# Spreading one group of a shared feed-forward over the tail of the attention stage

## The reference

```python
x = x + _L0_xattn_ref(_layernorm(x), ctx_512, Wq, Wkv_expand, Wout)      # 16 heads, causal
x = x + _L0_ffn_ref(_layernorm(x), ...)
# inside the feed-forward, xf is (3584, 512)
probs = softmax(xf @ gate_w.T); top_p, top_i = top_k(probs, 2)           # 8 experts
h = silu(xf @ expert_fc1[e].T) * (xf @ expert_fc2[e].T)                  # 352 wide
y = sum over the two chosen experts of top_p * (h @ expert_proj[e].T)
shared = (silu(xf @ shared_fc1.T) * (xf @ shared_fc2.T)) @ shared_proj.T # 1408 wide
y = y + sigmoid(xf @ shared_gate_w.T) * shared
```

## Time and profile before

| what | value |
|---|---|
| median of the runs | 1655.21 us (3 runs, 1654.87 to 1656.95) |
| the profiled execution | 1659.46 us, its span 1657.7 us |
| mean granted clock of TensorE | 0.975 |
| busy: PE, PEld, DVE, ACT, POOL | 94%, 80%, 52%, 37%, 33% |
| attention with its tail | to about 517 us |
| jobs | about 517 to 1004 us |
| shared feed-forward | about 1004 us to the end |

### The profile page before, as it was taken

One profiled execution on the slowest core, in us unless ns is written; L12 is line 12 of the kernel. 1 busy time (PEld: TensorE's weight loads), 2 busy tenths in 40 slices (PEclk: granted clock), 3 DMA queues, 4 the chain that ended last, 5 costly groups with the idle time before them and its releaser, 6 DMA issues.

```text
span 1657.7 us, 32046 instructions
## 1 busy us (share of the span) xinstructions
PE 1558.9 (94%) x11388; PEld 1328.0 (80%) x11388; DVE 860.6 (52%) x1661; ACT 613.0 (37%) x1946; POOL 552.2 (33%) x507
## 2 busy tenths in 40 slices
PE   4999999999833999999999999999999999999998
PEld 4788878888723999999999997888888888888886
DVE  4567667776554666666666664532323223333322
ACT  3778767777702333333333333321111111111111
POOL 4233445554454655556555531101010100000010
PEclk9999999999966999999999999999999999999999
DMA  5233434443324666666666655321120303030110
GB/s 168 76 92 91 91 85 91 89 87 70 85 45 144 235 243 237 238 237 237 245 242 237 237 189 204 128 88 40 47 77 4 109 18 102 25 102 25 51 52 26
DMA packets 82465, 202.71 MB, mean 122 GB/s; under 512 B 37424, under 2 KB 38448, under 8 KB 77648
## 3 DMA queue, kind: packets, MB, share of 16 engines
q1 hardware_dynamic: 70208, 168.44, 31.6%
q0 software_dynamic: 12176, 33.20, 6.2%
HBM read 153.64 MB, written 47.97 MB: 122 GB/s over the span
## 4 chain that ended last, share of the span: by engine, by line
PE 86%; issue 5%; DVE 3%; POOL 3%; DMA 2%; ACT 1%; another core or an unknown queue 0%; DVEq 0%; SPq 0%; POOLq 0%; ACTq 0%
PE psum L567 53%; PE psum L833 13%; PE psum L783 8%; PE psum L665 3%; PE psum L656 2%; PE psum L684 2%; PE psum L756 1%; POOL lists_dram L1071 1%; PE psum L693 1%; PE psum L673 1%; PE psum L716 1%; PE psum L580 1%; DVE wj_lo L1468 1%; DMA wj_raw<-in_w_experts 1%; PE psum L647 1%
## 5 line engine op out<-in xcount | busy, mean ns | idle before, releaser
L1179 POOL DMA_INDIRECT routed<-expert_out_dram,slot_b x56 | 55.3, 987 | 575.5 <-DVE slot_b L1530 383.4
L567 PE MATMUL psum<-nT_hi,ws_hi 128*128 128x512 f32 x616 | 243.2, 395 | 3.6 <-DVE nT_lo L1478 3.6
L567 PE MATMUL psum<-nT_hi,ws_lo 128*128 128x512 f32 x616 | 244.8, 397 | 0.0
L567 PE MATMUL psum<-nT_lo,ws_hi 128*128 128x512 f32 x616 | 244.2, 396 | 0.0
L1517 DVE TENSOR_TENSOR h_s<-psum,silu_s 128x512 f32<-128x512 f32 x77 | 53.3, 692 | 363.9 <-PE psum L567 359.7
L567 PE MATMUL psum<-gT_hi,wj_hi 128*128 128x256 f32 (+1 forms) x840 | 233.1, 278 | 1.2 <-DVE gT_lo L1449 1.2
L567 PE MATMUL psum<-gT_hi,wj_lo 128*128 128x256 f32 (+1 forms) x840 | 232.8, 277 | 0.0
L567 PE MATMUL psum<-gT_lo,wj_hi 128*128 128x256 f32 (+1 forms) x840 | 232.8, 277 | 0.0
L1141 POOL TENSOR_SCALAR wj_hi<-wj_raw 128x2816 fp32r<-128x2816 f32 x68 | 136.7, 2028 | 147.5 <-PE psum L783 102.2
L912 ACT ACTIVATE probs<-psum,minus_max 112x112 f32<-112x112 f32 x512 | 176.3, 432 | 3.1 <-DVE minus_max L1264 3.1
L1468 DVE TENSOR_TENSOR wj_lo<-wj_raw,wj_hi 128x2816 fp32r<-128x2816 f32 x70 | 170.3, 2435 | 7.6 <-POOL wj_hi L1141 4.5
(11 more groups left out here) (193 smaller groups left out, 3300.7 us busy)
## 6 DMA issues: line engine op xcount, KB each, us to landing
wj_raw<-in_w_experts SPq DMA_DIRECT2D x35, 2176.0 KB, 8.7
expert_out_dram<-y_c SPq DMA_DIRECT2D x35, 512.0 KB, 2.7
wj_raw<-in_w_shared SPq DMA_DIRECT2D x11, 768.0 KB, 4.4
x_in<-in_x SPq DMA_DIRECT2D x32, 224.0 KB, 4.0
x_res<-in_x SPq DMA_DIRECT2D x32, 224.0 KB, 3.1
x_dram<-x SPq DMA_DIRECT2D x32, 224.0 KB
normed_dram<-xn SPq DMA_DIRECT2D x32, 224.0 KB, 3.1
normedT_dram<-xn2T SPq DMA_DIRECT2D x32, 224.0 KB, 3.8
```

The costliest lines, as they stand in the source:

```text
L567: mm = pe.matmul(out_ap, u, v, start=(n == 0), stop=(n == last))
L1179: pool.indirect_dma_start(out=routed[:, b % 2, c, :], out_offset=None, in_=expert_out_dram, in_offset=bass.IndirectOffsetOnAxis(ap=slot_b[ ...
```

## The change

Group 0 of the shared feed-forward leaves the last stage. Its eleven chunks go onto TensorE, ScalarE and VectorE as `chunk0(0)` to `chunk0(7)` behind each of the steps (8, 0) to (9, 3), and as chunks 8 to 10 behind the last step. They have the same 24 + 12 matmuls as before, but one PSUM bank for each half of the hidden layer (5 and 7) and single buffers `silu_0` and `h_0`. The weights of each chunk are loaded and split for this group alone, and loaded and split again in the shared stage, whose first group is now group 1. The input of group 0 is loaded and split in the steps (7, 0) to (7, 3), one quarter in each. The result is added to `base0` in the first job, and stored back over the rows of `x1_dram` from which it came.

The table of jobs is made in two parts: `table_first` before chunk 6 and `table_second` after chunk 7. The 13 steps that compared a count with the multiples of 256 one after the other become one comparison over 128 x 104 elements and one sum. The barrier behind attention no longer waits for TensorE. The weights of job 0 are loaded in step (8, 2) into a buffer of their own and split between the chunks 8 and 9. In every step `aT_lo` now comes ahead of `choose` and `place` on VectorE.

The first group of the shared stage (group 1) adds the experts' outputs of two groups: those of group 0 in chunks 2 to 5, and its own, placed in chunk 8, two in chunk 9 and two in chunk 10. Between them SP stores group 0 and loads the `base` of group 1.

The core of the diff, for SP and TensorE:

```diff
+        def first_chunk(g, j):
+
+            return (g - NG) * TB + j if isinstance(g, int) and g >= NG else None
+
+        TAIL_CHUNKS = range(2 * TB, SC)
...
+            for i in range(2):
+                sp.dma_start(w0_raw[i], w_shared[i]).then_inc(w0_loaded[i], 16)
+
+            def load_chunk0(c):
+                if c + 2 < SC:
+                    sp.wait_ge(S["fc0_split"], c + 1)
+                    sp.wait_ge(S["pj0_split"], c + 1)
+                    sp.dma_start(w0_raw[c % 2], w_shared[c + 2]).then_inc(w0_loaded[c % 2], 16)
+
+            def tail_loads(g, j):
+                if g == NG and j == 0:
+                    sp.wait_ge(S["scores_done"], NB)
+                    sp.dma_start(base0[:, :, :], x1_dram[0:ST].rearrange("(b p) c -> p b c", p=P)).then_inc(S["base0_loaded"], 16)
+                    sp.dma_start(route_b0[:, :, :], route_groups[0]).then_inc(S["base0_loaded"], 16)
+                if g == NG and j == 2:
+                    wait_emptied(sp, NG, 1, "proj")
+                    sp.dma_start(wj_raws[0][:, :], w_experts[0]).then_inc(wjraw_loaded[0], 16)
+                load_chunk0(first_chunk(g, j))
 
...
+                    if isinstance(g, int) and g == NG - 1:
+                        if j == 0:
+                            for i in range(2):
+                                sp.wait_ge(x1_stored[i], 16 * 3)
+                                sp.wait_ge(xn2T_stored[i], 16 * 3)
+                            sp.wait_ge(S["route_stored"], 16 * 2)
+                        if j >= 2:
+                            sp.wait_ge(S["n0_split"], j - 1)
+                        sp.dma_start(n0_in[j % 2], normedT_dram[:, j, 0:ST]).then_inc(n0_loaded[j % 2], 16)
                     if j == 1 and before(g, NG - 1):
                         sp.wait_ge(S["ctx_split"], 2 * g + 2)
...
+                    if isinstance(g, int) and g >= NG:
+                        tail_loads(g, j)
...
@@ -472,6 +559,8 @@
                                  route_of(g - 1)[:, :, :]).then_inc(S["route_stored"], 16)
 
             groups(sp, body, 2)
+            for c in TAIL_CHUNKS:
+                load_chunk0(c)
...
             load_ids(0, 0)
             load_ids(1, 1)
-            sp.wait_ge(gathered[0], 16 * JT)
+            sp.wait_ge(S["pj0_split"], SC)
+            sp.wait_ge(S["fc0_split"], SC)
             load_weights(1, 1)
+            sp.wait_ge(S["base0_added"], SB)
+            sp.dma_start(x1_dram[0:ST].rearrange("(b p) c -> p b c", p=P), base0[:, :, :]).then_inc(S["base0_stored"], 16)
...
                 next_front(g, j)
 
+            def hidden0(c):
+                pe.wait_ge(S["fc0_split"], c + 1)
+                if c == 0:
+                    pe.wait_ge(S["n0_split"], KC)
+                    wait_emptied(pe, NG, 0, "sumT")
+                    wait_emptied(pe, NG, 0, "outT")
+                for half, (b, filled_0, emptied_0) in enumerate(((5, h1_filled, h1_emptied), (7, h2_filled, h2_emptied))):
+                    at_least(pe, emptied_0, c)
+                    pairs = []
+                    for k in range(KC):
+                        cols = slice((half * KC + k) * P, (half * KC + k + 1) * P)
+                        pairs.append(((fc0_hi[c % 2][:, cols], fc0_lo[c % 2][:, cols]), (n0_hi[:, k, :], n0_lo[:, k, :])))
+                    product(bank(b), pairs).then_inc(filled_0, 1)
+
+            def project0(c):
+                pe.wait_ge(S["hs0_split"], c + 1)
+                pe.wait_ge(S["pj0_split"], c + 1)
+                if c == 0:
+                    pe.wait_ge(S["exp_done"], 2 * NB)
+                w_hi, w_lo = pj0_hi[:, c % 3, :], pj0_lo[:, c % 3, :]
+                for j in range(SB):
+                    tok = slice(j * P, (j + 1) * P)
+                    a_hi, a_lo = hs0_hi[:, c % 2, tok], hs0_lo[:, c % 2, tok]
+                    for q, (u, v) in enumerate(((a_hi, w_hi), (a_hi, w_lo), (a_lo, w_hi))):
+                        mm = pe.matmul(bank(j), u, v, start=(c == 0 and q == 0), stop=(c == SC - 1 and q == 2))
+                mm.then_inc(S["proj0_done"], 1)
+
+            def chunk0(c):
+                hidden0(c)
+                if c:
+                    project0(c - 1)
+
             def body(g):
                 if is_first(g):
                     first_front()
                 for j in range(TB):
                     step(g, j)
+                    if isinstance(g, int) and g >= NG:
+                        if g == NG + 1 and j == 2:
+                            wait_emptied(pe, NG, 2, "router")
+                            pe.matmul(bank(6, P, EXPERTS), ones_f[:, :], chosen[:, TB, :], start=True, stop=True).then_inc(S["table_step"], 1)
+                        chunk0(first_chunk(g, j))
 
             pe.wait_ge(S["consts_made"], 11)
             groups(pe, body, 1)
 
-            pe.wait_ge(S["exp_done"], 2 * NB)
-            pe.wait_ge(S["choice_ready"], NG)
```

More of the change, by code:

```diff
@@ L134, in build_program @@
         jobs_i = keep("jobs_i", [1, 2 * NJOBS], I32)
+        job_ids = [keep(f"job_ids{i}", [P, JT], I32) for i in range(2)]
         prefer = keep("prefer", [P, TB, EXPERTS])
@@ L193, in build_program @@
         job_no = sa("job_no", [1, NJOBS, EXPERTS])
+        steps_f = sa("steps_f", [P, EXPERTS, CHUNKS - 1])
+        over = sa("over", [P, EXPERTS, CHUNKS - 1])
         job_w = sa("job_w", [1, NJOBS, EXPERTS])
         job_f = sa("job_f", [1, 4, NJOBS])
-        wkv_raw = sa("wkv_raw", [P, 2 * C])
+        v_sb = sa("v_sb", [SEQ, 2, C])
+        probs = sa("probs", [SEQ, 2, HEADS, SEQ])
+        probsT = sa("probsT", [SEQ, HEADS, SEQ])
+        rsum = sa("rsum", [SEQ, 2, HEADS])
+        rinv = sa("rinv", [SEQ, HEADS])
+        rinv_wide = sa("rinv_wide", [SEQ, HEADS, HD])
+        rinvT = sa("rinvT", [P, KC * SEQ])
+        attnT = sa("attnT", [P, KC * SEQ])
+        aT_hi, aT_lo = sa("aT_hi", [P, 2, KC, SEQ], F32R), sa("aT_lo", [P, 2, KC, SEQ], F32R)
+        x_res = sa("x_res", [SEQ, 2, C])
+        wout_hi, wout_lo = sa("wout_hi", [P, KC, C], F32R), sa("wout_lo", [P, KC, C], F32R)
+        sa("gap_a", [P, 1776])
+        n0_hi, n0_lo = sa("n0_hi", [P, KC, ST], F32R), sa("n0_lo", [P, KC, ST], F32R)
+        fc0_first = [sa(n, [P, 2 * KC * P], F32R) for n in ("fc0_hi0", "fc0_lo0")]
         phase_a.close()
@@ L336, in shared_groups, with is_opening, combine_groups @@
         def shared_groups(eng, body):
+            body(1)
+            body(2)
+            with eng.Fori(3, NS - 1) as g:
+                body(g)
+            body(NS - 1)
+        def is_opening(g):
+            return isinstance(g, int) and g == 1
+        def combine_groups(eng, body):
             body(0)
@@ L1404, in place, with table_first @@
                 dve.sem_inc(S["slots_ready"], 1)
+            table_chain = chain("table_step", 1)
+            def table_first():
+                dve.wait_ge(S["table_step"], 1)
+                link, _ = table_chain
+                link(dve.tensor_copy(jb["total"][:, :], bank(6, P, EXPERTS)))
+                link(dve.tensor_tensor(over[:, :, :], jb["total"][:, :].unsqueeze(2).to_broadcast([P, EXPERTS, CHUNKS - 1]), steps_f[:, :, :], ALU.is_gt))
+                link(dve.tensor_reduce(jb["n"][:, :], over[:, :, :], AX.X, ALU.add))
+                link(dve.tensor_scalar(jb["n"][:, :], jb["n"][:, :], 1.0, None, ALU.add))
+                link(dve.tensor_copy(jb["end"][:, :], jb["n"][:, :]))
+                for e in range(1, EXPERTS):
+                    link(dve.tensor_tensor(jb["end"][:, e:e + 1], jb["end"][:, e - 1:e], jb["n"][:, e:e + 1], ALU.add))
+                link(dve.tensor_tensor(jb["begin"][:, :], jb["end"][:, :], jb["n"][:, :], ALU.subtract))
@@ L1410, in body @@
                         route_z(g)
-            groups(dve, body, 1)
-            dve.wait_ge(S["table_step"], 1)
-            link, count = chain("table_step", 1)
-            link(dve.tensor_copy(jb["total"][:, :], bank(0, P, EXPERTS)))
-            link(dve.memset(jb["n"][:, :], 1.0))
-            for c in range(1, CHUNKS):
-                link(dve.scalar_tensor_tensor(jb["n"][:, :], jb["total"][:, :], float(c * JOB), jb["n"][:, :], ALU.is_gt, ALU.add))
-            link(dve.tensor_copy(jb["end"][:, :], jb["n"][:, :]))
```

294 lines of the change are left out of this document (182 added, 112 removed).

## The result

The changed kernel takes 1615.33 us, the median of 4 runs (1613.15 to 1618.94), against 1655.60 us for the kernel before in the same session (1654.87 to 1656.95): ratio 0.9758 [0.9739, 0.9777], 40.3 us less. The forecast was 1605 us in a range of 1596 to 1621. The time lies in the range and ten microseconds above the forecast. The profiled execution of after is the slowest of its four, 1618.94 us with a span of 1617.2 us. One execution of a kernel further down (`e8_after_early_adds`) took 2390 us at a mean granted clock of 0.65, where its other three have 0.99; nothing is read from it.

The account below looks back on a forecast made before the run. TensorE's work plus the hole from step (8, 0) to job 1 was taken as the bound. -92.1 + 37.6 + 1.0 + 3.5 = -50.0 us, from 1655.2 to 1605 us, range 1596 to 1621.

Parts of the forecast that it names:

- The hole: Stretch from step (8, 0) to job 1, 92.7 us of partly idle, low-clock TensorE; with group 0's chunks 130.3 us, +37.6.
- Pauses of (8, 0) to (8, 2): TensorE pauses that stay in the last attention steps: 6.2 us in sum, including 3.4 plus 0.7 us in (8, 0).
- Chunk 9: In the tail, TensorE stalls 3.7 us for weights split behind VectorE's table_second, plus 0.5 us for the low clock.
- First tokens: Before job 0: routing, scatters and gather end 36 us after h2 of chunk 5, TensorE arrives at 49; hidden, 13 to spare.
- Steps (7, 0) to (7, 3): Group 7's attention steps, paced by ScalarE: loading and splitting group 0's input costs +1.0 us, bounds 0 and 4.
- Reorder of aT_lo in earlier groups: Attention steps before the tail: aT_lo's new place leaves VectorE's sum the same, cost 0.
- Opening shared group: Group 1's end: late gathers and additions delay nT_lo, +3.5 us; as a rival (8%) in full, 8 us plus low clock.
- Removed group: Last stage: one shared group of 11 chunks leaves, -92.1 us.
- the slow clock through the tail: Rival, 3%: pauses before each chunk keep the clock low, each chunk costs 6.8 us more, 1680 us.
- the unfilled hole: Rival, 1%: TensorE meets the chunks only behind the routing chain, the hole stays 92.7 us, 1655 us or a little over.
- VectorE's queue: Rival, 12%: VectorE bounds several chunks, 2 us in each of four and 2 more at chunk 9, 1615 us.
- the late transfers: Rival, 10%: weights queued behind job 0's 2.2 MB, or tokens more than 13 us late, cost 4 to 10 us, 1612 us.

Follow-up runs that it names:

- `e8_after_early_adds`: Changed kernel with group 1's slots worked out in chunk 7 instead of 8 and its rows added in chunks 8 and 9 instead of 9 and 10: 1610.22 us, ratio 0.9742.
- `e10_three_mends_distance_32`: Kernel with tokens moved, group 7's splits behind the reciprocal and earlier adds, with gT 32 bytes lower (distance 32 from job weights, not 64): 1602.13 us against 1597.95.
- the mend: Changed kernel with VectorE's added splits of group 7 put behind the next step's reciprocal and maxima: 1610.61 us, ratio 0.9743.
- `e6_after_tokens_shifted_64`: Changed kernel with token tiles gT moved to byte 109728, 32 modulo 128 against the job weights' 96: 1606.89 us against 1654.32, ratio 0.9719.

## Why the prediction was right, and where it was off

- **The hole** (+37.6 foreseen, +36.7 measured). Right in mechanism and size, and the run with the chunks behind the last step shows that both halves of the mechanism are real. The idle time in it is 7.7 us where 10 to 12 were named, the low clock makes up part of the difference.
- **Pauses of (8, 0) to (8, 2)**. The wait on `rinv_wide` is 3.19 us where 2.06 + 0.7 = 2.8 was put down. What wasn't counted is the low clock behind it, 1.6 us. The prediction took from the earlier trace rows that a pause of 2.06 us costs nothing; another profile of the same instructions shows that it can, so that reading rested on one execution. The rule of the Trainium skill (TensorE: Matmul & The Clock Gate, "HAM oscillation — how this bites in real kernels"), by which work behind an idle gap starts cold, comes nearer, but not every trace agrees: behind the 3.19 us pause the clock fell in three profiles of four, behind the one in the opening group (2.63 to 2.88 us) in five of seven.
- **Chunk 9** (3.7 + 0.5 us foreseen, 0.41 measured). The term was mis-sized by its row. `table_second` took 4.8 us, not 8.4, because most of the gaps in the earlier trace rows belong to that one execution; the same steps take 4.8 to 5.4 us in every other profile. Here they are in the kernel before, shifted by 64 bytes:

```profile
494.36 0.17 DVE L1436 CAST jobs_i<-job_f 1x35 int32<-1x35 f32 x1
494.56 0.17 DVE L1437 CAST jobs_i<-job_f 1x35 int32<-1x35 f32 x1
494.88 0.17 DVE L1439 TENSOR_SCALAR jb_rows<-jb_begin 128x8 f32<-128x8 f32 x1
495.09 0.57 DVE L1441 TENSOR_TENSOR moved<-jb_rows,list_at 128x8 f32<-128x8 f32 x3
```

  The prediction named the case ("with the gaps ... gone it is 1.8") and did not take it. Its 1.8 is too long as well: with 4.8 us in place of 8.4 its own terms leave 0.1.
- **First tokens** (hidden with 13 us to spare foreseen, a wait of 0.70 us measured). The spare time was wrong by 13 us and the cost by 0.7, and the trace of after says where it went, counted from the end of h2 of chunk 5. TensorE came to the tokens after 45.2 us instead of 49, since the stall at chunk 9 was missing. The eight scatters and their landing took 18.0 us instead of 14.8. The ids and the gather took 15.5 us instead of 8.5, because the second gather landed 9.94 us after its issue, where the earlier trace rows have 3.42:

```profile
550.50 9.94 DMA xg<-normed_dram,job_ids
```

  Only `e10_three_mends_distance_32` has such a landing too (9.86 us, and a wait of 0.59). In both, SP issues the 2.2 MB of job 1's weights 0.26 us behind that gather. In the seven other profiles with the chunks between the steps it issues them 1.4 us or more behind it, and TensorE does not wait; where the landing is recorded, in six of them, it takes 3.6 to 4.7 us and leaves 5.7 to 8.5 us to spare. In the kernel before, SP waited for job 0's gathers before it issued these weights, and the change dropped that wait. That the weights hold up the gather is argued from this and not shown, since no run moves their issue alone.
- **Steps (7, 0) to (7, 3)** (+1.0 foreseen, about +4.4 measured in the profiles, most of it given back by the mend). "Three of the four quarters fit into waits" is the step that failed: they fit into VectorE's idle time of the step's end, but there they delay the reciprocal that opens the next one, and in most profiles the low clock follows. In the table this is hidden, since the profiled execution of before has one step of 17.97 us where every other profile has 13.8 (4.1 us, with 2.42 us in which TensorE waited for nothing that the profile shows).
- **Reorder of aT_lo in earlier groups** (0). Right within 0.3 us as far as the traces show: alone it gives 2 to 3 us, and the wait that became shorter is in the tail.
- **The jobs** (0 foreseen, +8.6 measured). This is the main miss, and no term of the sum had it: the diff's allocation lines were read as room, not as addresses.
- **Opening shared group** (+3.5 foreseen, +4.7 between silus). Right in its mechanism; the rest is the low clock behind the wait. In the two profiles in which the clock did not fall there, it is +3.0 us (14.0 and 14.1 against 11.05).
- **Removed group** (-92.1). Right; the later groups take 92.0 us each as before. In the profiles another 1.5 us was lost where the low clock held longer behind a 3.55 us wait at the start of the stage that both kernels have: the first 24 matmuls take 8.2 us there in after, 6.75 in before.

Of the rivals, the slow clock through the tail and the unfilled hole are out by the second row of the stretches, and VectorE's queue and the late transfers by TensorE's waits of 0.41 and 0.70 us; the opening group paid more than its term, but not in full. By the table the misses are -1.0, -0.9, +8.6 and +2.8 us, 9.5 in sum, and -50.0 + 9.5 = -40.5 us is the difference of the two profiled executions.

So the forecast is right in its mechanism, and the time is inside the range partly by luck: the range was made wide for other rivals, and the placement of the buffers, 8.5 us by itself, used up half of the room above the forecast. Without it (`e6_after_tokens_shifted_64`) the time is 1606.89 us.

## What to carry over

- When a change moves buffers, compare the time of stages that it doesn't touch, form by form: a mean of one matmul that rises from 277 to 288 ns without idle time points at placement, and a 64-byte tile tells.
- Work that fills idle time at the end of an engine's step stands ahead of the first instruction of its next step. Ask who waits for that one, and put the work behind it.
- A duration taken from one execution with gaps that no releaser explains (here 3.6 of 8.4 us) should be summed once with and once without them.
- What the low clock costs behind a pause needs more than one execution: here the same pause cost 1.6 us or nothing.
